# One RWKV stage in a hybrid network: heads one place later, output one group later, one addition moved to GpSimd

## The reference

```python
shifted = jnp.pad(x, ((0, 0), (1, 0), (0, 0)))[:, :T]
delta = shifted - x
low = jnp.tanh((x + delta * mu_x) @ W_x1).reshape(B, T, 5, PROJ_LR)
mus = jnp.einsum('blnr,dnr->blnd', low, W_x2) + x_bias
xr, xw, xk, xv, xg = [x + delta * mus[:, :, i] for i in range(5)]
r, k, v, g = xr @ W_r, xk @ W_k, xv @ W_v, xg @ W_g        # split in 16 heads
w = -jnp.exp(jnp.tanh(xw @ W_w1) @ W_w2 + b_w2)
o_t = einsum('bhk,bhkv->bhv', r_t, S) + einsum('bhk,hk,bhk,bhv->bhv', r_t, u, k_t, v_t)
S = jnp.exp(w_t)[..., None] * S + k_t[..., :, None] * v_t[..., None, :]
o = (o - mean) * rsqrt(var + EPS)                           # per head of 8 values
return ((o * gn_w + gn_b) * (g * sigmoid(g))) @ W_o
```

## Time and profile before

| | |
|---|---|
| median of 3 runs | 3604.78 us (3604.70 to 3609.48) |
| the profiled execution | 3612.22 us |
| its span | 3610.3 us (1.9 us lie around it) |
| mean granted TensorE clock, all stages | 0.902 |
| RWKV stage, first product kv of group 0 to that of group 15 | 51.19 to 471.26 us |
| last residual of the stage ends | 502.83 us |
| busy, all stages: PE, DVE, ACT, POOL | 87%, 66%, 47%, 33% |

### The profile page before, as it was taken

The page is one execution under the profiler, slowest core; times in us unless marked ns, Lnnn a source line. Parts: engine busy times, 40 slices in busy tenths (PEclk is TensorE's granted clock), DMA queues, the critical chain, the costliest instruction groups (busy, mean ns, idle before and its releaser), DMA issues. The chain is left out here.

```text
span 3610.3 us, 49465 instructions
## 1 busy us (share of the span) xinstructions
PE 3125.8 (87%) x16500; PEld 2058.4 (57%) x16500; DVE 2380.7 (66%) x5557; ACT 1703.2 (47%) x3659; POOL 1192.1 (33%) x1204
## 2 busy tenths in 40 slices
PE   6999964999872999997579996788979999999989
PEld 3454454888631444444568885687735555555557
DVE  5887775444595777775844444003479999999964
ACT  2434322333232799997133332212446666666644
POOL 3444331000132677775110001101224444444432
PEclk9999966999986999999589996557989999999999
DMA  3000012111032111101221100000000000000001
GB/s 109 1 1 1 1 35 69 36 36 34 16 112 78 29 29 29 30 26 39 60 73 36 45 1 1 0 0 26 1 1 1 1 1 1 1 1 1 1 4 44
DMA packets 106556, 91.24 MB, mean 25 GB/s; under 512 B 15501, under 2 KB 96147, under 8 KB 104000
## 3 DMA queue, kind: packets, MB, share of 16 engines
q1 hardware_dynamic: 104928, 87.25, 7.6%
q10 hardware_dynamic: 1376, 0.82, 0.1%
HBM read 57.60 MB, written 30.15 MB: 24 GB/s over the span
## 5 line engine op out<-in xcount | busy, mean ns | idle before, releaser
L2328 ACT ACTIVATE m_x_hT<-m_x_hid,wm_b 128x260 f32<-128x260 f32 x512 | 242.8, 478 | 436.3 <-PE m_x_hid L2250 436.3
L1326 POOL TENSOR_TENSOR c_tE<-c_tE,c_tDm 128x256 f32<-128x256 f32 x512 | 372.9, 730 | 138.9 <-ACT c_tE L1286 122.3
L1209 DVE TENSOR_REDUCE c_tM<-c_tpa 128x2 f32<-128x512 f32 x512 | 330.1, 682 | 131.1 <-PE c_tpa L1111 130.2
L1286 ACT ACTIVATE c_tE<-c_tpb 128x512 f32<-128x512 f32 x512 | 310.1, 607 | 43.0 <-PE c_tpb L1128 43.0
L2250 PE MATMUL m_x_hid<-m_x_xg,wm_w 128*128 128x260 f32 x1024 | 306.3, 386 | 11.0 <-ACT m_x_hT L2328 7.5
L2258 PE MATMUL m_x_yp<-m_x_hT,wm_w 128*128 128x260 f32 x1024 | 300.8, 383 | 0.0
L1662 POOL TENSOR_TENSOR b_wkv<-b_at,b_rec 128x512 f32<-128x512 f32 x128 | 163.3, 1276 | 306.0 <-DVE b_rec L1598 306.0
L1111 PE MATMUL c_tpa<-c_tK,c_Qm 96*128 96x256 f16 x1024 | 204.9, 283 | 49.8 <-DMA c_Qm<-aug_d 36.7
L79 POOL TENSOR_TENSOR rstd<-vareps,neg_half 128x4 f32<-128x4 f32 x80 | 86.4, 1080 | 460.4 <-DVE vareps L68 460.4
L2175 DVE TENSOR_SCALAR m_x_yT<-m_x_yp,wm_b 128x260 f32<-128x260 f32 x128 | 62.6, 489 | 256.1 <-PE m_x_yp L2258 256.1
L1267 ACT ACTIVATE c_tDm<-wc_pos,c_LD 128x128 f32<-128x128 f32 x512 | 209.2, 411 | 21.0 <-PEq L93 21.0
(11 more groups left out here) (322 smaller groups left out, 7363.0 us busy)
## 6 DMA issues: line engine op xcount, KB each, us to landing
m_x_ir<-idx_d SPq DMA_DIRECT2D x16, 1040.0 KB, 6.8
xn_d<-xn SPq DMA_DIRECT2D x32, 256.0 KB, 2.3
m_x_xs<-xn_d SPq DMA_DIRECT2D x16, 512.0 KB, 4.1
c_tK<-k_d SPq DMA_DIRECT2D x32, 192.0 KB
c_Qm<-q_d SPq DMA_DIRECT2D x128, 48.0 KB
wm_w<-in_m_w SPq DMA_DIRECT2D x2, 2048.0 KB, 9.4
gate_d<-c_pgate SPq DMA_DIRECT2D x16, 256.0 KB
q_d<-c_phi SPq DMA_DIRECT2D x32, 128.0 KB
```

The source lines that it names most:

```text
L1209: nc.vector.tensor_reduce(out=M[:, u % 2, 2 * h:2 * h + 2], in_=pa[:, h % 2], axis=AX.X, op=ALU.max).then_inc(s["max_done"], 1)
L1286: nc.scalar.activation(E[:, h % 8].rearrange("p a q -> p (a q)"), pb[:, h % 2, :], ACT.Exp).then_inc(s["exp_done"], 1)
L1326: nc.gpsimd.tensor_tensor(diag, diag, Dm[:, u % 2, h:h + 1, :].to_broadcast([P, 2, P]), ALU.mult).then_inc(s["dmul_done"], 1)
L2328: nc.scalar.activation(hT[:, e % 2, j, :], hid[:, c % 2, 0:QW], ACT.Gelu, bias=w["m_b1"][:, c:c + 1]).then_inc(s["gelu_done"], 1)
```

## The change

It does three things, and the waits follow them:

1. `heads(g-1)` is done in pass g, behind `values(g)` and `mixes(g+1)`, instead of `heads(g)` at the end of pass g. The tile rS has two copies for that.
2. `gated`, `out` and `residual` of a group come one pass later (of g - 2 in pass g); gg has three copies; `square`, `root` and `affine` on ScalarE, `variance`, `normalise`, `gate` and `bonus_value` on VectorE take other places in their pass, and `turn_back` goes to the end of TensorE's. The second low_rank product moves from bank 4 to bank 0.
3. The receptance's x is added by GpSimd (`add_x(g+1, 4)` between `read(g, 1)` and `read(g, 2)`), and the two half products L619 are gone.

The diff, without the places that only count to 4 where they counted to 3 (decay_low, plain_value and gate on TensorE):

```diff
@@ -307,3 +307,3 @@
         S = sb("S", [P, VQ, 2, T + 1])
-        rS = sb("rS", [P, VQ, GW])
+        rS = sb("rS", [P, 2, VQ, GW])
         ruk = sb("ruk", [HK, GW])
@@ -311,3 +311,3 @@
         th = sb("th", [P, GW])
-        gg = sb("gg", [P, 2, GW])
+        gg = sb("gg", [P, 3, GW])
         sq = sb("sq", [P, GT * HA, VD])
@@ -335,3 +335,3 @@
         BANK = {"m0": 0, "m1": 1, "m2": 2, "m3": 3, "m4": 0, "w": 0, "vv": 1, "gate": 2, "c": 3, "low0": 3,
-                "turn": 4, "nT": 4, "y": 4, "low1": 4}
+                "turn": 4, "nT": 4, "y": 4, "low1": 0}
         at = {name: bank[:, b, :] for name, b in BANK.items()}
@@ -420,4 +420,4 @@
                 dve.wait_ge(s["th_done"], p + 1)
-                at_least(dve, s["z_done"], p - 1)
-                nc.vector.scalar_tensor_tensor(out=gg[:, p % 2, :], in0=th[:], scalar=1.0, in1=at["gate"],
+                at_least(dve, s["z_done"], p - 2)
+                nc.vector.scalar_tensor_tensor(out=gg[:, p % 3, :], in0=th[:], scalar=1.0, in1=at["gate"],
                                                op0=ALU.add, op1=ALU.mult).then_inc(s["gg_done"], 1)
@@ -450,3 +450,3 @@
                 at_least(dve, s["y_done"], p)
-                nc.vector.tensor_tensor(z[:], nt[:], gg[:, p % 2, :], ALU.mult).then_inc(s["z_done"], 1)
+                nc.vector.tensor_tensor(z[:], nt[:], gg[:, p % 3, :], ALU.mult).then_inc(s["z_done"], 1)
 
@@ -457,3 +457,5 @@
 
-            for g in range(-3, NG + 1):
+            for g in range(-3, NG + 2):
+                if has(g - 2):
+                    gated(g - 2)
                 if has(g):
@@ -464,12 +466,7 @@
                     mix_out(g + 1, 1)
-                if has(g - 1):
-                    variance(g - 1)
                 if has(g):
-                    bonus_key(g)
                     scan(g, 0)
+                    bonus_key(g)
                 if has(g + 1):
                     mix_out(g + 1, 2)
-                if has(g - 1):
-                    normalise(g - 1)
-                if has(g + 1):
                     mix_out(g + 1, 3)
@@ -477,16 +474,20 @@
                 if has(g):
-                    for v in range(1, VQ):
-                        scan(g, v)
-                if has(g - 1):
-                    gated(g - 1)
+                    scan(g, 1)
+                if has(g - 2):
+                    residual(g - 2)
                 if has(g):
-                    bonus_value(g)
+                    scan(g, 2)
+                    scan(g, 3)
+                if has(g - 1):
+                    variance(g - 1)
                 if has(g + 2):
                     mix_in(g + 2)
-                if has(g + 1):
-                    gate(g + 1)
                 if has(g - 1):
-                    residual(g - 1)
+                    normalise(g - 1)
                 if has(g + 3):
                     moments(g + 3)
+                if has(g + 1):
+                    gate(g + 1)
+                if has(g):
+                    bonus_value(g)
             dve.wait_ge(s["res_done"], NG)
@@ -520,4 +521,4 @@
                     pool.wait_ge(s["r_out"], p + 1)
-                    at_least(pool, s["oc_done"], p)
-                nc.gpsimd.tensor_tensor(seq(rS[:, v, :]), S[:, v, :, 0:T], seq(rr[:, p % 2, :]), ALU.mult).then_inc(s["rs_done"], 1)
+                    at_least(pool, s["oc_done"], p - 1)
+                nc.gpsimd.tensor_tensor(seq(rS[:, p % 2, v, :]), S[:, v, :, 0:T], seq(rr[:, p % 2, :]), ALU.mult).then_inc(s["rs_done"], 1)
 
@@ -531,2 +532,8 @@
                     add_x(g + 1, 3)
+                if has(g):
+                    read(g, 1)
+                if has(g + 1):
+                    add_x(g + 1, 4)
+                if has(g):
+                    read(g, 2)
                 if has(g + 2):
@@ -534,4 +541,3 @@
                 if has(g):
-                    for v in range(1, VQ):
-                        read(g, v)
+                    read(g, 3)
                 if has(g + 3):
@@ -543,3 +549,3 @@
                 if v == 0:
-                    pe.wait_ge(s["xi_done"], 3 * p + 2)
+                    pe.wait_ge(s["xi_done"], 4 * p + 2)
                     pe.wait_ge(s["r_out"], p + 1)
@@ -555,3 +561,2 @@
                     pe.wait_ge(s["low_out"], 2 * p + 2)
-                    at_least(pe, s["ew_done"], p)
                 elif j == 1:
@@ -567,3 +572,3 @@
                 pe.wait_ge(s["xn_done"], p + 1)
-                at_least(pe, s["low_out"], 2 * p)
+                at_least(pe, s["res_done"], p - 3)
                 for i in range(GT):
@@ -615,9 +620,5 @@
             def receptance(p):
-                pe.wait_ge(s["dm_done"], 5 * p + 5)
+                pe.wait_ge(s["xi_done"], 4 * p + 4)
                 pe.wait_ge(s["tw_out"], p + 1)
-                for half in range(2):
-                    nc.tensor.matmul(at["r"][:, half * T:(half + 1) * T], lhsT=w["a_wr"][:], rhs=x(p)[:, half, :],
-                                     start=(half == 0), stop=False, skip_group_check=True)
-                nc.tensor.matmul(at["r"], lhsT=w["a_wr"][:], rhs=xi[:, 0, :], start=False, stop=True, skip_group_check=True)\
-                    .then_inc(s["r_done"], 1)
+                nc.tensor.matmul(at["r"], lhsT=w["a_wr"][:], rhs=xi[:, 0, :], start=True, stop=True).then_inc(s["r_done"], 1)
 
@@ -637,3 +638,3 @@
                     for i in range(GT):
-                        nc.tensor.matmul(oc[:, i, :], lhsT=rS[:, v, i * P:(i + 1) * P], rhs=w["a_sel"][:, v, :],
+                        nc.tensor.matmul(oc[:, i, :], lhsT=rS[:, p % 2, v, i * P:(i + 1) * P], rhs=w["a_sel"][:, v, :],
                                          start=(v == 0 and i == 0), stop=False, skip_group_check=True)
@@ -649,7 +650,6 @@
                 nc.tensor.matmul(at["low0"], lhsT=w["a_wx1"][:, 0:P], rhs=xm[:], start=True, stop=True).then_inc(s["low_done"], 1)
-                at_least(pe, s["res_done"], p - 2)
-                pe.wait_ge(s["xT_ready"], p + 1)
+                at_least(pe, s["ew_done"], p)
                 nc.tensor.matmul(at["low1"], lhsT=w["a_wx1"][:, 32:32 + P], rhs=xm[:], start=True, stop=True).then_inc(s["low_done"], 1)
 
-            for g in range(-3, NG + 1):
+            for g in range(-3, NG + 2):
                 if has(g):
@@ -660,2 +660,6 @@
                         mixes(g + 1, j)
+                if has(g - 2):
+                    out(g - 2)
+                if has(g - 1):
+                    heads(g - 1)
                 if has(g + 2):
@@ -665,5 +669,2 @@
                     plain_value(g + 1)
-                if has(g - 1):
-                    turn_back(g - 1)
-                if has(g + 1):
                     key(g + 1)
@@ -676,5 +677,3 @@
                 if has(g - 1):
-                    out(g - 1)
-                if has(g):
-                    heads(g)
+                    turn_back(g - 1)
                 if has(g + 2):
@@ -697,4 +696,4 @@
                 act.wait_ge(s["turned"], p + 1)
-                at_least(act, s["xi_done"], 3 * (p - 1))
-                at_least(act, s["r_done"], p - 1)
+                at_least(act, s["xi_done"], 4 * (p - 1))
+                at_least(act, s["k_done"], p - 1)
                 nc.scalar.copy(x(p), seq(at["turn"])).then_inc(s["xT_ready"], 1)
@@ -760,3 +759,3 @@
                 if has(g - 1):
-                    root(g - 1)
+                    square(g - 1)
                 if has(g + 2):
@@ -767,3 +766,3 @@
                 if has(g - 1):
-                    affine(g - 1)
+                    root(g - 1)
                 if has(g + 1):
@@ -775,4 +774,4 @@
                     layernorm(g + 3)
-                if has(g):
-                    square(g)
+                if has(g - 1):
+                    affine(g - 1)
                 if has(g + 2):
```

More of the change, by code:

```diff
@@ L464, in _ @@
                     mix_out(g + 1, 1)
-                if has(g - 1):
-                    variance(g - 1)
                 if has(g):
+                    scan(g, 0)
                     bonus_key(g)
-                    scan(g, 0)
                 if has(g + 1):
                     mix_out(g + 1, 2)
-                if has(g - 1):
-                    normalise(g - 1)
-                if has(g + 1):
                     mix_out(g + 1, 3)
@@ L477, in _ @@
                 if has(g):
-                    for v in range(1, VQ):
-                        scan(g, v)
-                if has(g - 1):
-                    gated(g - 1)
+                    scan(g, 1)
[4 more added lines that the diff above has]
+                    scan(g, 3)
+                if has(g - 1):
+                    variance(g - 1)
+                if has(g + 2):
+                    mix_in(g + 2)
+                if has(g - 1):
+                    normalise(g - 1)
+                if has(g + 3):
+                    moments(g + 3)
+                if has(g + 1):
+                    gate(g + 1)
                 if has(g):
                     bonus_value(g)
-                if has(g + 2):
```

(11 more changed lines are left out.)

## The result

The changed kernel takes 3618.11 us (median of 7, 3616.84 to 3619.58) against 3606.22 (median of 7, 3602.51 to 3609.48): ratio 1.0033, 95% interval 1.0022 to 1.0044. It is 12 us slower; 10 less was forecast.

The account below looks back on a forecast made before the run. It took a loop of waits as the bound: VectorE waiting for values behind heads, 28.66 us a turn. Groups 10.9 less, start 0.9 less, tail 2 more: net 9.8 off the median 3604.8 gives 3595.0 us, range 3577 to 3614.

Parts of the forecast that it names:

- low_rank may not start before bonus_value has ended (bank 3), then 0.15 + 1.72 + 1.06 = 2.9: TensorE's chain from the end of VectorE's pass to the next outer: 2.9 us after 24.7, so 27.6.
- TensorE's slack of 2.2: TensorE's pass: turn_back follows normalise at 21.9, low_rank is free to start at 24.7; slack 2.2 us.
- lasts 1.25 (half of 2.50; 1.1 in the other parity): GpSimd's first addition beside the first scan pair: 1.25 us long, so that scan waits to about 5.65.
- cv at 24.7: End of bonus_value on VectorE, 24.7 us after the first outer: 18.7 of work and 6.0 of stalls.
- Group 0: First group, without residual, normalise or gated: 25.4 us against 24.0, since bonus_value closes the pass and the addition is there.
- The tail: Behind the last group's start, heads(15) waits for out(14), after normalise, affine and gated: 2 us more, bounds 0 and 4.
- the start: Ahead of group 0, where the receptance's halves are on the path: 0.9 us less.
- the two chains and their distance of 0.2: Pass end to next outer: low_rank's chain on TensorE 27.6, ScalarE's through affine and gated 27.8, which decides by 0.2.
- the stall of the added addition: VectorE's scans beside GpSimd's new addition: each GpSimd instruction in the way priced at 0.93 to 1.1 us.
- The port costs more: Rival, GpSimd against VectorE: all reads, additions and delta in the way, 2.4 us a group more, 3629; chance 0.18.
- the port costs less: Rival, GpSimd beside PSUM work more often: stalls 4.5 us, a group 26.3, 3574; chance 0.17.
- Nothing is left: Rival on ScalarE: root's wait for variance makes gate's tanh late by 0.7, 28.5 us a group, 3604; chance 0.15.

Follow-up runs that it names:

- Experiment 1: Changed kernel with two unused 128x512 products between turn_back and low_rank, filling TensorE's idle stretch: ratio 1.0003 to the kernel before.
- Experiment 7: Kernel of experiment 6 with the rows of xT 272 floats apart instead of 257: ratio 0.9869 to the kernel before.
- experiment 4: Changed kernel with affine ahead of layernorm on ScalarE and bonus_value ahead of moments and gate on VectorE: ratio 0.9921 to the kernel before.
- experiment 5: Kernel of experiment 1 with affine ahead of layernorm, bonus_value left where it is: ratio 0.9985 to the kernel before.
- experiment 2: Changed kernel with part 3 alone undone, TensorE adding the receptance's x again: ratio 0.9967 to the kernel before.
- experiment 3: Kernel before with part 3 alone, GpSimd adding the receptance's x: ratio 1.0094 to the kernel before.
- experiment 6: Changed kernel with the two moves of experiment 4 and part 3 undone: ratio 0.9888 to the kernel before.

## Why the prediction was wrong

By its own sum, forecast and then the profile: ahead of group 0, -0.9 and -3.6; group 0, +1.4 and +4.6; groups 1 to 13, -10.8 and +5.3; group 14, -1.4 and -0.1; the last group with its tail, +2 and +3.7. Together -9.8 and +10.0. Of the miss of 19.8, groups 1 to 13 hold 16.1.

- **The step that failed: "low_rank may not start before bonus_value has ended (bank 3), then 0.15 + 1.72 + 1.06 = 2.9".** These were the durations of before, at full clock. In the slow group they measured 0.15 + 2.99 + 1.55 = 4.69. The change put TensorE's idle stretch, 2.2 us, directly ahead of low_rank and values, and the products behind it ran at half clock in every second group. Experiment 1, which fills the stretch, gets 10.4 of the 16.1 back; why the other groups kept the full clock stays open. The prediction spoke of the clock only for the tail, and counted TensorE's slack of 2.2 as harmless. The mean clock of groups 1 to 13 is the same before and after; where it falls is not.
- **"lasts 1.25 (half of 2.50; 1.1 in the other parity)"** was seen, and then one walk made for both. It started from rows of the slow parity and yet came out at the fast one's value: cv at 24.7, as against 24.68 and 25.40. That the fast group is met so closely is in part luck. The slow one has four additions 0.18 longer, 0.7 a group, every second group: 4 to 5 us over the 13 groups. Experiment 7 shows that this goes with the place of x. The last 1 us of the 16.1 is group 13, forecast at 26.0 and measured at 26.97, in experiment 1 as well; why wasn't traced.
- **Group 0** had 25.4 forecast and took 28.6. TensorE, from the receptance to the first product of values:

```profile
63.35 1.13 PE L623 MATMUL a_vp<-a_xi,wa_wr 128*128 128x512 f32 x2 [1.39 <-POOL a_xi L516]
70.81 2.04 PE L650 MATMUL a_bank<-a_xm,wa_wx 128*128 128x512 f32 x2 [6.33 <-DVE a_cv L417]
72.65 1.91 PE L652 MATMUL a_bank<-a_xm,wa_wx 128*128 128x512 f32 x2
```

It waits 6.33 us for cv with no heads in between, and low_rank runs at half clock (pitch 1.8). Experiment 1 leaves this pass unfilled, and it took 28.59 there as well. How much of the 3.2 is clock alone wasn't tried.
- **The tail** was +3.7 instead of +2, within its bounds; the start -3.6 instead of -0.9. Experiments 1, 4 and 5, which differ from the changed kernel in nothing ahead of group 0 but the order of a step or two, had their first kv product at 46.02, 48.11 and 48.13, as against its 47.56, so about 2 us of this term is not a matter of the kernel. The rest was not traced.
- **Right:** the two chains and their distance of 0.2 (experiment 5); the stall of the added addition, 0.85 to 1.03 (experiments 2 and 3) at 0.93 to 1.1 forecast for one instruction in the way; L619's products worth nothing on the loop (experiment 2: the group distance moves by what the scans lose).
- **The rivals.** "The port costs more" came out on the right side for another reason: cv ends at 25.4 of a slow pass, 0.7 over the walk, and at 24.7 of a fast one, both under the 1.2 over it from which that rival decides. By the same two figures "the port costs less" did not happen. "Nothing is left", by the tanh, did not happen either: gate waits for nothing.

## What to carry to other kernels

When a change opens an idle stretch on TensorE, look at what runs right behind it. If that is on the loop, price it at half clock too; with the same mean clock and an idle stretch of the same length (2.2 us), the place decided here whether it cost 1.5 us in every second group or 0.5 at most. Where two engines wait for the end of a pass, look for what stands ahead of each closing step without being needed by it: bonus_value ahead of the moments and gate, together with affine ahead of layernorm, took 40 us off the changed kernel, some 10 of them by the clock. And an addition on GpSimd that runs beside VectorE's scans costs VectorE 0.85 to 1.03 us; it costs the kernel that much only where VectorE is on the loop (0.3 to 0.5 in experiment 6).

## What was not expected of the hardware

- Two unused products of 0.86 us each in every pass take 10.4 us off groups 1 to 13 (ratio 1.0033 to 1.0003), which then run at a granted clock of 1.00 and not 0.97.
- The same GpSimd addition (the third of a pass) takes 1.09 or 1.27 us in the kernel before, in turn, and 1.43 or 1.61 beside the scans of experiment 6; with the rows of x 272 floats apart and not 257 it takes 1.43 in both (experiment 7). Reads and delta do not differ by parity. Which property of the address does it wasn't tried.
